# Scaling both states' output weights on ScalarE, with the factors formed by VectorE

## The reference, cut to what matters

```
def step(carry, x):
    S_f, S_s = carry
    S_f = fdt * S_f;  S_s = sdt * S_s
    err_f = vt - kt @ S_f;  err_s = vt - kt @ S_s
    S_f = S_f + bt * outer(kt, err_f);  S_s = S_s + bt * outer(kt, err_s)
    S_fc = _cap(S_f + rf * S_s)          # S / max(1, |S| / 64)
    S_sc = _cap(S_s + rf * S_f)
    ot = fgt * (qt @ S_fc) + sgt * (qt @ S_sc)
    return (S_fc, S_sc), ot
```

## Time and profile before

| | us |
|---|---|
| median of 3 runs | 1874.05 (1873.61 to 1875.43) |
| the profiled execution | 1869.62 |
| its span | 1867.5 |
| the recurrence block in it | 805.95 to 1066.38 |

### The profile page before, as it was taken

One profiled execution on the slowest core, in us unless ns is written; L12 is line 12 of the kernel. 1 busy time (PEld: TensorE's weight loads), 2 busy tenths in 40 slices (PEclk: granted clock), 3 DMA queues, 4 the chain that ended last, 5 costly groups with the idle time before them and its releaser, 6 DMA issues. The chain is left out here.

```text
span 1867.5 us, 22300 instructions
## 1 busy us (share of the span) xinstructions
PE 1538.5 (82%) x7255; PEld 1144.2 (61%) x7255; DVE 1199.0 (64%) x2644; ACT 713.3 (38%) x1364; POOL 96.1 (5%) x261
## 2 busy tenths in 40 slices
PE   6999999999799999349100089489999999999998
PEld 3888888888667767213000088466666666666664
DVE  4366555665336786999999756455655555556555
ACT  2343343333355455201000222155555555555552
POOL 0000000000000000022112100130000000000003
PEclk9999999999899999779555579689999999999999
DMA  3211011100241441450100231525605514426004
GB/s 119 80 35 33 18 34 34 34 24 10 95 66 44 81 80 41 70 180 1 45 0 0 69 83 36 192 96 209 208 18 203 208 56 165 160 72 207 13 17 141
DMA packets 134201, 152.94 MB, mean 82 GB/s; under 512 B 64096, under 2 KB 84960, under 8 KB 134112
## 3 DMA queue, kind: packets, MB, share of 16 engines
q1 hardware_dynamic: 128384, 137.68, 24.4%
q0 software_dynamic: 2560, 8.39, 1.4%
q10 hardware_dynamic: 3168, 5.77, 0.8%
HBM read 250.25 MB, written 31.33 MB: 151 GB/s over the span
## 5 line engine op out<-in xcount | busy, mean ns | idle before, releaser
L1758 DVE TENSOR_TENSOR gl<-w_gu,gh 128x2048 fp32r<-128x2048 f32 x138 | 290.5, 2106 | 6.8 <-ACT gh L1697 6.7
L1697 ACT CAST gh<-w_gu 128x2048 fp32r<-128x2048 f32 x138 | 242.0, 1755 | 41.8 <-PEq L1413 19.2
L1652 PE MATMUL bank<-w_d,hT 128*128 128x512 f32 x506 | 242.2, 597 | 8.8 <-ACT hT L1720 8.0
L1791 DVE TENSOR_TENSOR hid<-silu,bank 128x256 f32<-128x256 f32 x138 | 55.0, 399 | 264.6 <-ACT silu L1709 264.6
L1629 PE MATMUL bank<-gh,xh 128*128 128x512 f32 (+1 forms) x552 | 217.7, 394 | 1.7 <-DVE xl L1749 1.4
L1631 PE MATMUL bank<-gh,xl 128*128 128x512 f32 (+1 forms) x552 | 205.9, 373 | 0.0
L1630 PE MATMUL bank<-gl,xh 128*128 128x512 f32 (+1 forms) x552 | 205.5, 372 | 0.0
L1229 PE MATMUL bank<-o_v,xnT 128*128 128x64 f32 x256 | 36.1, 310 | 177.9 <-DMA o_v<-scratch_v_rows 177.9
L1229 PEld LDWEIGHTS bank<-o_v,xnT 128*128 128x128 f32 x256 | 35.8, 227 | 178.7 <-DMA o_v<-scratch_v_rows 178.7
L1652 PEld LDWEIGHTS bank<-w_d,hT 128*128 128x128 f32 x506 | 91.7, 189 | 82.0 <-issue 56.9
L1709 ACT ACTIVATE silu<-bank 128x256 f32<-128x256 f32 x138 | 50.6, 367 | 218.3 <-PE bank L1631 216.3
(11 more groups left out here) (296 smaller groups left out, 3097.1 us busy)
## 6 DMA issues: line engine op xcount, KB each, us to landing
w_gu<-in_gate_proj SPq DMA_DIRECT2D x46, 1024.0 KB
w_gu<-in_up_proj SPq DMA_DIRECT2D x46, 1024.0 KB
w_d<-in_down_proj SPq DMA_DIRECT2D x46, 1024.0 KB
w_gu<-in_gate_proj SPq DMA_DIRECT2D x23, 768.0 KB
w_gu<-in_up_proj SPq DMA_DIRECT2D x23, 768.0 KB
w_d<-in_down_proj SPq DMA_DIRECT2D x23, 768.0 KB
ctx_raw<-in_ctxT SPq DMA_DIRECT2D x32, 385.5 KB, 3.7
scratch_x_slots<-r_outw SPq DMA_DIRECT2D x1, 5888.0 KB, 19.3
```

The source lines that it names most:

```text
L1652: mm = pe.matmul(bank, hT[n % 2][:, c, :], w_d[:, b * (BLK // P) + c, :], start=(b == 0 and c == 0), stop=(b == NB - 1 and c == cs[-1]))
L1697: nc.scalar.copy(gh[n % RING][:, :, :, 0:bw].rearrange("p k a f -> p (k a) f"), w_gu[:, :, :, b * BLK:b * BLK + bw].rearrange("p k a f -> ...
L1758: nc.vector.tensor_tensor(gl[n % RING][:, :, :, 0:bw].rearrange("p k a f -> p (k a) f"), w_gu[:, :, :, b * BLK:b * BLK + bw].rearrange("p ...
L1791: nc.vector.tensor_tensor(hid[n % 2][:, 0:bw], silu[n % 2][:, 0:bw], ps[GU_BANK + n % 3][:, bw:2 * bw], ALU.mult).then_inc(hid_done, 1)
```

## The change

The factors `cg` are formed by DVE, right behind the reciprocal and the third group of sums. ACT scales each state and group of `psi` by its factor: 8 operations per step, each over m elements, with the factor as a per-partition operand. They are called `gate_states(t)` and stand between root t and the copy of the gate projection. POOL keeps the sum and the product with the table. `cg` and `outs` get two buffers each. ACT waits for POOL's step t - 2 before it writes `outs` again, and DVE for ACT's step t - 2 before it writes `cg` again.

```diff
-        cg, outs, outsum = sb("r_cg", [P, 2, SG]), sb("r_outs", [P, 2, SG, N]), sb("r_outsum", [P, SG, N])
+        cg, outs = [sb(f"r_cg{i}", [P, 2, SG]) for i in range(2)], [sb(f"r_outs{i}", [P, 2, SG, N]) for i in range(2)]
+        outsum, cg_ready, states_gated = sb("r_outsum", [P, SG, N]), sem("r_cgr"), sem("r_gated")
...
-        POOL_STEPS = 4
+        POOL_STEPS = 2
...
-                    pool.wait_ge(psi_ready, t + 1)
-                    nc.gpsimd.tensor_tensor(cg[:, :, :], cap[u][:, :, :], gt[:, :, 3:5, t].rearrange("p s e -> p e s"),
-                                            ALU.mult).then_inc(out_done, 1)
+                    pool.wait_ge(states_gated, t + 1)
+                    if t:
+                        pool.wait_ge(out_done, n)
+                    nc.gpsimd.tensor_tensor(outsum[:, :, 0:m], outs[t % 2][:, 0, :, 0:m], outs[t % 2][:, 1, :, 0:m], ALU.add).then_inc(out_done, 1)
                     pool.wait_ge(out_done, n + 1)
-                    nc.gpsimd.tensor_tensor(outs[:, :, :, 0:m], psi[u][:, :, :, 0:m], bc(cg[:, :, :, None], [2, SG, m]),
-                                            ALU.mult).then_inc(out_done, 1)
-                    pool.wait_ge(out_done, n + 2)
-                    nc.gpsimd.tensor_tensor(outsum[:, :, 0:m], outs[:, 0, :, 0:m], outs[:, 1, :, 0:m], ALU.add).then_inc(out_done, 1)
-                    pool.wait_ge(out_done, n + 3)
                     nc.gpsimd.tensor_tensor(outw[:, :, 0:m, t], outsum[:, :, 0:m], G[:, :, 0:m, 1, t], ALU.mult).then_inc(out_done, 1)
...
+                def gate_states(t):
+
+                    act.wait_ge(cg_ready, t + 1)
+                    if t >= 2:
+                        act.wait_ge(out_done, (t - 1) * POOL_STEPS)
+                    for e in range(2):
+                        for s in range(SG):
+                            ins = nc.scalar.activation(outs[t % 2][:, e, s, 0:t + 1], psi[t % PSI][:, e, s, 0:t + 1], ACT.Copy,
+                                                       scale=cg[t % 2][:, e, s:s + 1])
+                    ins.then_inc(states_gated, 1)
+
                 for t in range(N):
                     act.wait_ge(nm_ready, t + 1)
                     nc.scalar.activation(root[:, :, :], nm[:, :, :], ACT.Sqrt).then_inc(root_ready, 1)
+                    gate_states(t)
...
+                    summed = sums(2)
+                    dve.wait_ge(psi_ready, t + 1)
+                    if t >= 2:
+                        dve.wait_ge(states_gated, t - 1)
+                    tt(cg[t % 2][:, :, :], cap[u][:, :, :], gt[:, :, 3:5, t].rearrange("p s e -> p e s"), ALU.mult).then_inc(cg_ready, 1)
                     if nxt == N:
                         break
-                    summed = sums(2)
-                    dve.wait_ge(psi_ready, t + 1)
```

## The result

The changed kernel takes 1893.59 us (median of 4 runs, 1892.59 to 1897.15) against 1873.98 us (4 runs, 1873.61 to 1875.43) before: ratio 1.0098, 95% interval 1.0077 to 1.0119. It is slower by 19.6 us by the medians; 1896 was forecast, with a range from 1887 to 1903.

The account below looks back on a forecast made before the run. DVE alone was taken to bound the recurrence block. Terms of 15.6 + 2.2 + 2.0 + 2.6 = +22.4 us on the median of 1874.05 gave 1896.5, predicted as 1896 us, range 1887 to 1903.

Parts of the forecast that it names:

- What bounds the block: Recurrence block: DVE alone sets the pace, so removing work from POOL gives nothing by itself.
- The wait for `outs`: Step 3: root 3 queues behind gate_states(2), which waits for POOL's step 0 and the blanking DMA; +15.6 us.
- Later waits: Steps after the stall: ACT's group fits before the next root, 2.1 of 2.9 us, so roots are in time.
- `cg` on DVE: Steps 3 to 30: the added 8-element product costs DVE 0.08 us each, +2.2 us.
- What POOL does to DVE: Recurrence steps: POOL's two remaining operations delay DVE's products by 9.2 us, against 7 us before; +2 us.
- The end of the block: After step 31's reciprocal: cg and ACT's last group delay the table load and Silus; +2.6 us.
- A: Rival, chance 0.10: the stall comes, but POOL's 7 us delay of DVE shrinks to 2; +15.4 us, 1889.5 us.
- B: Rival, chance 0.05: ACT too slow in each step, roots of steps 4 to 8 late; 1901 to 1903 us.
- C: Rival, chance 0.02: scaled copies need another table than the roots; at least 37 us more, 1933 us.
- D: Rival, chance 0.05: the blanking DMA lands before 817.2 us, so nothing holds root 3; -2.2 us, 1872 us.
- One sign that was named against the forecast: Steps after the stall: lengths more than 0.3 us apart from those before would show the forecast wrong.

Follow-up runs that it names:

- The small buffers: The changed kernel, with the scaled weights of steps 0 to 7 in eight small buffers of their own; 1877.16 us, ratio 1.0003 to the kernel before.
- the blanking source of its own: The changed kernel, with the blanking DMAs reading from a tensor of their own so POOL does not wait for them; 1877.76 us, ratio 1.0010.
- the two quiet kernels: The kernel before and the changed kernel, each with POOL's operations per step replaced by a one-column memset; root 3 to 31 takes 229.81 and 232.34 us.
- POOL held: Changed kernel with early buffers, cg behind the decay factors, early Silus, and POOL's step t waiting for DVE's last product of step t + 1; 1870.68 us.
- the factors behind: The changed kernel with early buffers for steps 0 to 7, and cg placed behind the decay factors instead of in front; 1877.67 us.

## Why the prediction was right, step by step

**What bounds the block: right.** DVE does. Taking work from POOL gave nothing by POOL's own time.

**The wait for `outs`: right, in place, cause and size.** Forecast +15.6 us with root 3 at 835.4; measured root 3 at 835.47, +15.55 us behind root 0. The small buffers and the blanking source of its own each took it away, and four buffers halved it. Two errors inside the term cancel: the group takes 1.60 us where 1.9 was worked out (a scaling adds 0.19 us and not 0.225), and POOL started at 833.37, 0.4 us later than before, for which the rows give no reason. That these 0.3 and 0.4 us cancel is luck.

**Later waits: right, with more room than stated.** Doubling the group to some 3 us cost the steps behind the stall 0.4 us in all. DVE never waited for POOL but for 0.7 us, once, for a memset at the block's start; nothing rests on it.

**`cg` on DVE: right.** +2.2 forecast, +2.53 between the two quiet kernels, 0.08 us in nearly every step; 0.2 of it is the open delay of step 4, which `cg` alone does not bring.

**What POOL does to DVE: mechanism right, size wrong, and here is the term that was mis-sized.** The 7 us of before were right (7.00). For after I took half of each operation's duration in every step, 9.2 us; it is 5.51. So the term is -1.5 us where +2 was forecast, within its bounds of -6 to +7. In steps 7 to 25 two operations cost only 0.15 us a step where 0.33 was assumed: in the rows of step 20 one lies beside a reduction and costs nothing, and the other costs one product 0.13 us. In steps 26 to 30 both lie beside two-input instructions of DVE, in step 28 the mixing of the states, and they cost 0.46 us, which is half of their durations. Rows of one place were carried to another. The Trainium skill's rule (SBUF — State Buffer, Who interferes with whom) that the later one is blocked for the whole of the other's instruction would, with recorded durations, have doubled the term; the step-28 rows show 0.16 and 0.29 us of delay to DVE beside POOL operations that alone take 0.45 and 0.5 us, so whole recorded durations overstate it here. The same section of the Trainium skill states that on this chip `tensor_reduce` never contends with GpSimd; the rows of step 27 with POOL held agree, 0.68 and 1.21 us for sums beside POOL as without it.

**The end of the block: right within half a us.** Forecast +2.6, measured +2.17. The Silus end 2.49 us later behind root 31 (the last group takes 1.80 us where 2.0 was worked out), and 0.3 us of that did not count, since before it was the stores that ended last.

The sum of the block was forecast +22.4 us and is +18.8; 3.5 of the 3.6 us between are the contention term. A (stall with DVE relieved of POOL) named the right direction for that term but not its size. B fell with the doubled group, C with the absence of any table load between roots and scalings, D with root 3. One sign that was named against the forecast did show: step 4 is 0.39 us and steps 27 to 30 are 0.48 to 0.59 us longer than before, where more than 0.3 was to count. It points at the contention term and at step 4, not at the stall, so the block's sum held while the course of its steps did not.

## What to carry to other kernels

When work moves to another engine, read which queue it enters and what stands behind it there: the added operations of 1.6 us were harmless, but the wait in front of them put a root of the critical chain behind a DMA that only POOL had waited for. A ring of eight buffers had hidden that start, a ring of two exposed it, and two more buffers took two steps off it. Where two engines hold each other up, what counts is which instructions lie beside each other and not how many there are. Holding the helper's work until the main engine is in its sums gave 3 us without any other change (interval 0.4 to 5), and would have given more if no clamp stood between the sums: look at every instruction beside the helper's work, the small ones too.

## What the runs showed that was not expected

The price of an operation of POOL to DVE depends on its place by a factor of three: 0.15 us for two in steps 7 to 25, 0.46 us for two in steps 26 to 30. Moving the start of POOL's three operations behind one group of sums cost some 3 us, by what is left of the time when the added instruction is taken off.

Step 4 is 0.2 to 0.4 us longer in every kernel in which ACT scales the states (4.16 us with two buffers, 4.05 with small ones, 3.98 with the factors behind), and not where VectorE forms the factors without ACT's part (3.85) or before (3.77). DVE stands 0.25 us behind its own reciprocal there, once. The cause stays open.

What follows the block differs by up to 7.5 us between executions of code that is the same, so a change of this size in the recurrence is better read from its own block than from the whole.
